# Macaron block on one core: the tokens of stages 2 and 3 are transposed by DMA instead of TensorE, and GpSimd's tile-wide steps move to VectorE

## The reference

```python
x = x + 0.5 * _L0_ffn_ref(_layernorm(x), ...)     # feed-forward
x = x + _L0_attn_ref(_layernorm(x), w_attn, w_o)  # windows of 128 tokens
x = x + 0.5 * _L0_ffn_ref(_layernorm(x), ...)     # the same weights again

# _L0_ffn_ref, for its input x:
thought = layer_norm(x)[:, -1, :] @ agg_w + agg_b           # the last token of each batch only
for _ in range(4):
    t = gelu(layer_norm(thought) @ d1_w + d1_b)             # 1024 -> 4096
    thought = thought + (t @ d2_w + d2_b)                   # 4096 -> 1024
broadcast = (thought @ bc_w + bc_b)[:, None, :]
gate = sigmoid(x @ gate_w + gate_b)                         # all tokens, 1024 x 1024
return layer_norm(x + gate * broadcast) * out_gamma + out_beta

# _L0_attn_ref: q, k, v = x @ w_attn.T; each window of 128 tokens sees itself and the one before
sim = where(keep, q @ k.T / 128, 0); out = relu(sim) ** 2 @ v; return out @ w_o.T
```

## Time and profile before

| | |
|---|---|
| Median of 3 runs (lowest, highest) | 2239.18 us (2238.72, 2240.87) |
| The profiled execution's own time | 2231.3 us |
| Its span, first to last instruction | 2230.1 us |
| PE, DVE, ACT, POOL busy | 2101.3, 1137.8, 624.8, 493.8 us |
| Mean granted TensorE clock | 0.977 |

### The profile page before, as it was taken

How to read it: one execution, slowest core, us unless ns; L and a number is a source line. 1 busy time by engine, 2 the same in 40 slices (tenths; PEclk the granted TensorE clock), 3 DMA queues, 4 the chain that set the end, 5 groups by cost and what they waited for, 6 DMA issues and landing times.

```text
span 2230.1 us, 31260 instructions
## 1 busy us (share of the span) xinstructions
PE 2101.3 (94%) x12384; PEld 1096.8 (49%) x12384; DVE 1137.8 (51%) x2076; ACT 624.8 (28%) x931; POOL 493.8 (22%) x409
## 2 busy tenths in 40 slices
PE   8987799899999999968998999999999998999996
PEld 3333334334443456644655555666665564444443
DVE  2322224444444444546555444543543516999998
ACT  0657223323233322223332212212112103322331
POOL 0000000000000222211211212221211203666665
PEclk9999899999999999989999999999999999999998
DMA  9679698988899522267868677678686533222211
GB/s 352 224 260 378 231 357 302 362 297 333 326 340 385 193 76 76 97 234 272 293 266 311 260 254 287 221 278 300 243 315 264 186 149 135 95 95 95 95 76 57
DMA packets 142096, 522.25 MB, mean 234 GB/s; under 512 B 15920, under 2 KB 16128, under 8 KB 141568
## 3 DMA queue, kind: packets, MB, share of 16 engines
q1 hardware_dynamic: 141952, 520.26, 63.0%
HBM read 406.94 MB, written 113.26 MB: 233 GB/s over the span
## 4 chain that ended last, share of the span: by engine, by line
PE 82%; DMA 6%; DVE 5%; ACT 3%; issue 2%; SPq 1%; POOL 1%; ACTq 0%; DVEq 0%
PE product_banks L944 58%; PE product_banks L975 9%; PE product_banks L1071 4%; PE thought_acc L1142 4%; PE turn_banks L953 3%; PE thought_acc L1132 3%; DMA thought_units<-in_d_w 2%; DMA thought_row<-in_d_w 1%; DMA thought_units<-parts_scratch 1%; ACT thought_units L1309 1%; DVE bn_parts L1348 1%; DVE thought_units L1636 1%; DMA wide_b<-x_scratch 1%; DMA wide_a<-in_w_attn 1%; ACT thought_units L1325 1%
## 5 line engine op out<-in xcount | busy, mean ns | idle before, releaser
L944 PE MATMUL product_banks<-gate_arena,arena 128*128 128x512 f16 x1536 | 352.2, 382 | 0.0
L944 PE MATMUL product_banks<-gate_arena,wide_a 128*128 128x256 f16 x3072 | 345.4, 273 | 1.7 <-DVE gate_arena L1361 1.7
L944 PE MATMUL product_banks<-wide_b,gate_arena 128*128 128x512 f16 x1536 | 342.9, 380 | 0.0
L944 PE MATMUL product_banks<-wide_a,arena 128*128 128x512 f16 x1536 | 338.2, 381 | 0.0
L944 PEld LDWEIGHTS product_banks<-gate_arena,wide_a 128*128 128x128 f16 x3072 | 298.1, 98 | 55.4 <-issue 20.5
L1700 POOL TENSOR_TENSOR token_stats<-stats,minus_half 128x1 f32<-128x1 f32 x96 | 84.2, 877 | 808.2 <-DVE stats L1355 792.4
L975 PE MATMUL product_banks<-wide_a,wide_b 128*128 128x512 f32 x512 | 237.6, 611 | 13.3 <-ACT wide_a L1208 7.3
L944 PEld LDWEIGHTS product_banks<-gate_arena,arena 128*128 128x128 f16 x1536 | 145.0, 98 | 212.1 <-issue 56.1
L944 PEld LDWEIGHTS product_banks<-wide_b,gate_arena 128*128 128x128 f16 x1536 | 146.0, 98 | 188.7 <-issue 22.8
L944 PEld LDWEIGHTS product_banks<-wide_a,arena 128*128 128x128 f16 x1536 | 150.5, 98 | 175.7 <-issue 2.1
L1348 DVE BATCH_NORM_STATS2 bn_parts<-arena 128x6 f32<-128x512 f32 x256 | 164.1, 683 | 2.6
(11 more groups left out here) (152 smaller groups left out, 2089.2 us busy)
## 6 DMA issues: line engine op xcount, KB each, us to landing
thought_units<-parts_scratch SPq DMA_DIRECT2D x268, 512.0 KB, 6.0
thought_units<-in_d_w SPq DMA_DIRECT2D x148, 512.0 KB, 6.7
thought_row<-in_d_w SPq DMA_DIRECT2D x76, 512.0 KB, 6.5
arena<-in_x SPq DMA_DIRECT2D x64, 512.0 KB, 8.3
parts_scratch<-thought_units SPq DMA_DIRECT2D x64, 512.0 KB, 5.0
x_scratch<-arena SPq DMA_DIRECT2D x64, 512.0 KB, 6.2
gate_scratch<-arena SPq DMA_DIRECT2D x32, 512.0 KB, 8.3
arena<-gate_scratch SPq DMA_DIRECT2D x32, 512.0 KB, 8.7
```

Source lines behind the costliest of these rows:

```text
L944: mm = pe.matmul(bank, left(i, k), right(j, k), start=(n == 0), stop=(n == 3 * KD - 1))
```

## The change

Five things change.

1. The tiles of stages 2 and 3 are no longer transposed by PE. After `prep_h1` (and after `h3`) ACT copies the tile to f16 as it lies (high), DVE makes the low part from SBUF (`prep_low`, `low_3`), both parts as one row of 2048 f16 numbers, and SP issues one `dma_start_transpose` of 128x2048 f16 (512 KB), SBUF to SBUF: 32 in stage 2, 32 in stage 3. Stage 1's `turn` and `wo_turn` stay as they are.
2. The gate times the broadcast row and the addition of half of beta, in both stages, go from POOL to DVE. POOL keeps its steps of one column.
3. The moments before stage 3 (`x2_stats`) are taken in stage 2 from the tile in `xs_slots`, right behind its `collect`, and no longer from the loaded tile in stage 3.
4. The moments of the last norm are taken otherwise: DVE's addition in `sum_3` also yields the row's sum, DVE makes minus the mean of it, and ACT squares with that bias and sums in passing (`square_3`), where DVE had BATCH_NORM_STATS2 and aggregate.
5. Order and places: `sum_3` and `end_3` now follow one tile behind instead of two; the stage 2 preparation is paced at 1.3 items for each PE piece over products and attention together (0.9 before, over the products, then the turns at 1.0); the gate weights are loaded back (`load_3`, 4 MB) behind the last group's `q` and no longer behind its `v`; groups 0 and 1 are transposed into slots of `thought_units`.

```diff
 def plan_prep(n):
-        out += [("prep_h", u), ("rest",), ("rest",), ("prep_y", u), ("rest",), ("prep_stats", u),
-                ("rest",), ("rest",), ("x1_store", u), ("prep_h1", u), ("rest",)]
+        out += [("prep_h", u), ("rest",), ("prep_beta", u), ("prep_y", u), ("rest",), ("prep_x1", u),
+                ("prep_stats", u), ("rest",), ("x1_store", u), ("prep_h1", u), ("rest",), ("prep_low", u),
+                ("group_turn", u)]
...
 def plan_stage_2(first, last):
-        out += paced(plan_products(n), plan_prep(n + 1) if more else [], 0.9, PE_PIECES)
-        out += paced(plan_attention(n), plan_group_turn(n + 1) if more else plan_prepare_3(), 1.0, PE_PIECES)
+        if more:
+            out += paced(plan_products(n) + plan_attention(n), plan_prep(n + 1), 1.3, PE_PIECES)
+        else:
+            out += plan_products(n) + paced(plan_attention(n), plan_prepare_3(), 1.0, PE_PIECES)
...
 def plan_stage_3():
+        if n >= 1:
+            out.append(("sum_3", n - 1))
         if n + 4 < TILES:
             out.append(("x3", n + 4))
...
+        out += [("gate_3", n, 0, 0)]
+        if n >= 1:
+            out.append(("square_3", n - 1))
+        if n + 2 < TILES:
+            out += [("low_3", n + 2), ("turn_3", n + 2)]
+        out += [("gate_3", n, 0, 1)]
+        if n >= 1:
+            out.append(("var_3", n - 1))
+        out += [("beta_3", n), ("gate_3", n, 0, 2), ("gate_3", n, 1, 0)]
+        if n >= 1:
+            out.append(("end_3", n - 1))
...
     def sync_program():
                     sp.wait_ge(gate_out[u % GATE_RING], 16 * (u // GATE_RING + 1))
+                    if n:
+                        sp.wait_ge(group_in[s], 16 * n)
                     sp.dma_start(pg_slots[s], gate1_dram[row_of(TILE_OF[u]), :]).then_inc(pg_in[s], 16)
+            elif kind == "group_turn":
+                u, = a
+                n, i = divmod(u, GROUP)
+                sp.wait_ge(lows_made, u + 1)
...
+                sp.dma_start_transpose(
+                    group_of(n).rearrange("p h k t -> p (h k) t")[:, :, i * P:(i + 1) * P],
+                    pg_slots[u % PREP_RING].bitcast(F16)).then_inc(group_in[i], 16)
...
-                sp.wait_ge(product_full, BANK_AT[("v", GROUPS - 1, 1, 1)] + 1)
+                sp.wait_ge(product_full, BANK_AT[("q", GROUPS - 1, KD - 2)] + 1)
...
+            elif kind == "turn_3":
+                n, = a
+                s = n % PAIR3_RING
+                sp.wait_ge(lows3_made, n + 1)
+                if n >= PAIR3_RING:
+                    sp.wait_ge(product_full, BANK_AT[("gate_3", n - PAIR3_RING, 1)] + 1)
...
+                sp.dma_start_transpose(as_pair(pair3_slots[s]).rearrange("p h k t -> p (h k) t"),
+                                       low3_slots[s].bitcast(F16)).then_inc(pair3_in[s], 16)
...
     def vector_program():
+            elif kind == "prep_h":
...
+                dve.wait_ge(pg_in[u % PREP_RING], 16 * (u // PREP_RING + 1))
+                dve.tensor_tensor(gb, gb, thought_row[:, GROUP_OF[u // GROUP][0], :], ALU.mult).then_inc(gate_spread, 1)
...
             elif kind == "sum_3":
...
+                dve.wait_ge(gated_3, 2 * (n + 1))
+                dve.tensor_tensor(gb, gb, thought_row[:, ORDER_3[n] // NT, :], ALU.mult).then_inc(own.up(), 1)
...
+                dve.scalar_tensor_tensor(out=hb, in0=gb, scalar=1.0, in1=hb, op0=ALU.mult, op1=ALU.add,
+                                         accum_out=st[:, 0:1]).then_inc(y3_made, 1)
...
     def scalar_program():
+            elif kind == "square_3":
...
+                act.activation(squares3, h3_slots[n % H3_RING], ACT.Square, bias=st[:, 3:4],
+                               accum_out=st[:, 1:2]).then_inc(squared_3, 1)
```

More of the change, by code:

```diff
@@ L402, in plan_attention @@
     out += [("score", n, i, third) for i in (1, 0) for third in range(3)]
[L403 removed]
+    for c, (at, *_) in enumerate(COLLECTS):
+        if at == n:
+            out += [("collect", c, 0), ("collect", c, 1), ("x2_stats", c)]
     return out
```

275 lines of the change are left out of this document (143 added, 132 removed).

## The result

The changed kernel takes **2156.9 us** (median of 4 runs, 2152.1 to 2165.4), the kernel before 2239.2 beside it: a ratio of 0.9635, 95% interval 0.9603 to 0.9668. The forecast was 2184 with a range from 2158 to 2236.

A forecast was written before the change was run, and what follows sets the result against it. PE was taken to bound stage 2, PE and DVE together stage 3. Savings of 22 + 18 + 9 + 6.5 = 55.5 us, set against the median 2239.2, gave 2184 us, range 2158 to 2236.

The forecast's parts named there:

- Term A: Stage 3's period falls from 11.24 to 10.55 us a tile over 32 tiles, DVE last to be ready: -22 us.
- The best case of -28: Stage 3 at best, with its period set by PE's 10.36 us a tile: -28 us.
- DVE keeps stage 3 at its old period: Rival: stage 3 gains nothing, as DVE still sets its pace; 2206 us, chance 0.15.
- Term B: Stage 2: PE transposes removed, worth 28 us, less 10 us charged for four kinds of new waits: -18 us.
- (4): Stage 2 charge: 32 more DMAs of 512 KB on DMA engines at 0.76 and more; part of 10 us for four.
- (1): Stage 2 charge: DVE gets more steps, some 9 us in a group of 66; part of 10 us for four.
- (2): Stage 2 charge: DVE, not POOL, waits for the gate tile, holding evictions and thought's steps; part of 10 us for four.
- (3): Stage 2 charge: SP waits for the low half, with the thought's next loads behind it; part of 10 us for four.
- The price of a transpose: One DMA transpose in stages 2 and 3: about 4 us taken, between 2.6 and 20.8 us.
- The rival of slow transposes: DMA transposes above some 8 us set the pace of stages 2 and 3; about 2850 us at 20.8 each; chance 0.13.
- Term C: Handover to stage 3: earlier moments and gate-weight load remove 10.8 us, 2 left for the first tile's chain: -9 us.
- Term D: End of the kernel: one tile of DVE work behind PE, 8.6 us, instead of two, 15.3 us: -6.5 us.

The follow-up runs named there:

- Runs 2 and 3: Changed kernel with one more DVE product per stage 3 tile, result unused: 256 columns in the first, 2161.1 us; 1024 columns in the second, 2176.0 us.
- run 5: Changed kernel with stage 3's product with the row and addition of half of beta back on POOL: 2217.1 us, 0.9880 of the kernel before.
- run 6: Changed kernel with the last norm's moments back on DVE by BATCH_NORM_STATS2, no square on ACT: 2185.7 us, 0.9744 of the kernel before.
- run 1: Changed kernel with eight PE transposes of a constant put back for each of 30 stage 2 tiles, 240 in all, nobody waiting for them: 2177.1 us.
- run 10: Changed kernel with two more plain 512 KB stores to unused memory behind every stage 2 transpose, 64 in all: 2188.3 us.
- run 9: Changed kernel with stage 2's product of gate and row and its addition of half of beta back on POOL: 2164.0 us.
- run 11: Changed kernel with stage 2's preparation paced at 1.0 item for each PE piece instead of 1.3: 2183.3 us.
- run 4: Changed kernel with each stage 3 DMA transpose issued three times, the second and third into unused space: 2183.7 us.
- run 8: Changed kernel with the 4 MB `load_3` of gate weights back behind the last group's `v`: 2164.3 us.
- run 14: The kernel before, unchanged, executed once more for a second profile: 2244.4 us.
- run 7: Changed kernel with stage 3's product and beta back on POOL and the last norm's moments back on DVE: 2249.1 us, 1.0035 of the kernel before.

## Why the prediction missed, by its own steps

**Term A, -22, measured -26.** PE's 10.36 us are right, and so is the walk through DVE but for its small steps. I put DVE at 10.55, "still last to be ready, by a hair"; it is 9.89, and PE sets the period. The mean and the variance hold up the next step by 0.07 us each, with 0.18 of wait for ACT, where I took 0.6; the sum in passing costs 0.08 and is within the 1.27 of its step, where I took 1.33 and 0.17. The other steps differ by less than 0.1 each, 0.15 together. Runs 2 and 3 show the room: 256 columns fit into the 0.47 us, and with 1024 the period is 9.89 and one more step. The step of `end_3` that I took at 1.39, since POOL's tile-wide work beside it "goes", is shown by runs 5 and 6: 3.43 with POOL, 1.28 without. The best case of -28 was out of reach here: 30 of the 32 tiles' turns lay within stage 3 on PE, and 30 by 0.87 are the 26 us. The other two lay in the handover. The rival "DVE keeps stage 3 at its old period" falls, though run 6 alone brings it back, at 11.23.

**Term B, -18, measured -30: the step that failed.** The 28 us of turns stood up as work, nearly: 240 of the 256 turns lay within the stage, 26 us, and PE's busy time fell by 23 (0.44 for four; 0.87 for eight in run 1, 17 to 20 us net for 240). What failed is "I charge 10 us for all four" waits. The net of all waits was -7, not +10. Of the four, (4) came, 8 us more of waits for the thought's units, for which run 10 speaks for DMA room without excluding SP's queue. (1) and (2) didn't come. Together they had the wrong sign: POOL's tile-wide work, which goes to DVE, had held up DVE's own steps. I had seen that in stage 3, in the 2.74 us of `end_3`, and left it out of term B at nothing. The waits for DVE in the thought shrank by 9 us, and run 9, which gives POOL its two steps back, brings 3 to 10 us of them back (27.2 against 17.1 to 23.9) and makes stage 2 6 to 11 us longer. (3) was not tried by itself; it is the part of (4) that run 10 leaves open. And I counted only what the change adds to waits, none of those that go: PE's waits for the turns' DVE steps, 4 us within the stage, and 3 us at `key_weights`, which no run isolates. The cover that I named, "score and collect left", holds for pace 1.3 alone: at 1.0 (run 11) it costs 26 us.

**The price of a transpose** was right for stage 3, 4.3 us to land where I took about 4; in stage 2 it was 6.7 (median). The cost to the DMA engines is less, 2.9. My sum of 4 plus 2.9 us in a period took landing for occupancy: for run 4 it gives 14.9 us for a tile, and 11.24 were measured. The rival of slow transposes falls, and with it the Trainium skill's 1309 ns for 128x128 ("VectorE: DVE Perf Modes", "The three transpose paths") as a pace: 16 such blocks land in 4.3 us. Its other figure, 261 GB/s ("DMA: Bandwidth & Descriptors", "Latency and other measured facts"), is nearer, and still above this case: 524 KB in 2.9 to 3.2 us are 164 to 181 GB/s.

**Term C, -9, measured -9.5**, is right in size and partly by luck. I had taken 9.2 us of waits and 1.57 of the first tile as gone and left 2 for the new chain. The waits fell by 5.5, from 9.2 to 3.71, and run 8 shows that the earlier load did it. The 1.57 did not go: 32 tiles by 10.36 are 331.5 us, stage 3 took 333.3, and the granted clock was 0.92 from 1815 to 1825 us. In their place came what I had not put here: the turns of the first two tiles, 3.0 us before (1846.61 to 1848.52 and 1851.48 to 1852.60), and 1.0 us of the `collect` matmuls (9.76 to 8.75). **Term D, -6.5, measured -6.8**, with the 8.6 us of one tile as worked out. **Stage 1 to 2, 0, measured +0.5**: PE waits 3.93 us there for the first transposes, where it waited 3.14 and 1.67 for DVE.

**The rest is the base.** 12.3 us of the miss are term B, 4.1 term A, 0.8 C and D, less 0.5 for stage 1; 10 are the difference between the profiled executions (72.2) and the medians (82.2). I set the sum against the median, which is right only if the profiled execution loses the same as a typical one. The one I had was the fastest of 40 executions of this kernel (2231.3; the others 2231.8 to 2249.1), at a mean clock of 0.977; run 14, at 0.973, was slower by 13. For 36 of the 40 the clock is known: 0.969 to 0.977, on average 0.973, so that the one I read had the highest. The changed kernel's eight executions had 2152 to 2165 us at 0.977 to 0.980, on average 0.979, and its profile had 0.979 as well. So a typical execution of before loses more clock than the one I read, and a typical one of the changed kernel does not. All eight of the changed kernel lie at or above the highest of the kernel before, which speaks for the change as the reason; in the handover, where PE waits less, the clock rose from 0.84 to 0.99. Runs in which PE waits in every tile of stage 3 have less (0.974 to 0.976 in run 5, 0.967 to 0.972 in run 7). No run isolates what keeps the clock up.

## What to carry to other kernels

When a change removes an instruction from the engine that bounds a stage, list the waits that stood with it as well as those that may come; a charge for new waits alone is one-sided. An effect that is seen in one stage (here POOL's hold on DVE's steps) is to be priced in every stage that the change touches. Work that is taken from a second engine can be worth more than its own time where it ran beside two-input steps of the first: look for one operation that has two durations in the trace. And before a sum is set against a median, see where the profiled execution lies among the runs and what its granted clock was.

## What the runs showed of the hardware

- **DVE and POOL shut each other out.** A DVE step with two SBUF inputs takes 1.27 us by itself, 2.74 in the kernel before and 3.43 in run 5, where it starts with POOL's 2.35 us and ends 1.09 after it. POOL isn't slower there (2.35 and 2.37), but it is where DVE starts first (3.33 in run 9). Small steps pay too: 845 ns for 128x8 in run 9, 227 without POOL's tile-wide work. The Trainium skill says so ("SBUF — State Buffer", "SBUF: two separate sides": an exclusive lock between GpSimd and a DVE op with two SBUF inputs, held for the whole instruction), and the trace agrees.
- **A transpose of 128x2048 f16 SBUF to SBUF** lands in 4.3 us in stage 3 (6.7 in the busier stage 2) and takes 2.9 to 3.2 us of all DMA engines, an estimate from the DMA shares. It goes in small packets (those under 512 B rise from 15,920 to 149,040 for 64 of them, 2,080 each), and holds the issuing SP for 1.8 us in stage 3 and 4.6 in stage 2 (medians).
- **A sum in passing** on a DVE step shows as 0.08 us more, on an ACT step as 0.19 (at 2151.81 in the end's timeline). From DVE's step with the sum to the next is 1.27 us, from the product ahead of it 1.26.
- **The spread of executions goes with the granted clock**: 0.969 to 0.977 over 36 executions of the kernel before, 0.977 to 0.980 over eight of the changed one. By a straight line through each, with clocks rounded to a thousandth, a thousandth is worth some 2 and some 3 us.
